# Second layer of a two-layer sequence model: one PSUM bank for the sums, step sizes ahead of the gates, small GpSimd operations on ScalarE, another order on the way to the experts

## The reference, cut to what matters

```python
# selective scan (d_model 256, d_inner 512, 16 states), per sequence
x_ssm, res = split(x @ W_in.T)                      # 512 + 512
x_ssm = silu(conv4(x_ssm) + b_conv)
B_C   = (x_ssm @ W_x.T)[..., 512:]                  # 16 values a token
dt    = softplus(x_ssm @ W_dt.T + b_dt)             # step size
h     = exp(dt * A) * h + dt * B * x_ssm            # scan over tokens, 512 x 16 states
y     = h.sum(-1) + D * x_ssm
out   = (y * silu(res)) @ W_out.T
# sorted experts: two groups of 32 experts, top 2 of each group
xs = x2[tokens sorted by expert]
ys = (silu(xs @ wg[e]) * (xs @ wu[e])) @ wd[e]      # 256 -> 128 -> 256
out = zeros.at[tok].add(ys * weight)                # both groups, averaged
```

## Time and profile before

| | us |
|---|---|
| median of 3 runs | 4872.82 (4868.73 to 4875.76) |
| the profiled execution | 4861.3 |
| its span in the trace | 4859.5 |
| TensorE matmul busy | 4278.9 (88%) |
| VectorE busy | 3722.3 (77%) |
| GpSimd busy | 3037.6 (63%) |
| ScalarE busy | 2516.5 (52%) |

### The profile page before, as it was taken

How to read it: one execution, slowest core, us unless ns; L and a number is a source line. 1 busy time by engine, 2 the same in 40 slices (tenths; PEclk the granted TensorE clock), 3 DMA queues, 4 the chain that set the end, 5 groups by cost and what they waited for, 6 DMA issues and landing times. The chain is left out here.

```text
span 4859.5 us, 59293 instructions
## 1 busy us (share of the span) xinstructions
PE 4278.9 (88%) x19350; PEld 2834.2 (58%) x19350; DVE 3722.3 (77%) x5916; ACT 2516.5 (52%) x4871; POOL 3037.6 (63%) x1970
## 2 busy tenths in 40 slices
PE   5689999999999999998988889888988888499993
PEld 1355555555556655565655566555655665388883
DVE  6887777778788878775149988888988898555676
ACT  1344334334333434433468777777777777155552
POOL 3455555555555545554158889888888888555552
PEclk7899999999999999999999999999999999699997
DMA  4233332333332333333112221111222111496787
GB/s 146 80 107 104 109 100 92 110 98 111 109 104 90 105 105 104 105 109 100 39 67 75 80 73 70 70 69 69 86 87 75 69 67 68 162 248 209 260 282 278
DMA packets 304193, 545.54 MB, mean 112 GB/s; under 512 B 31504, under 2 KB 148496, under 8 KB 294928
## 3 DMA queue, kind: packets, MB, share of 16 engines
q1 hardware_dynamic: 276240, 466.09, 29.5%
q0 software_dynamic: 27648, 75.67, 4.3%
HBM read 422.72 MB, written 118.92 MB: 111 GB/s over the span
## 5 line engine op out<-in xcount | busy, mean ns | idle before, releaser
L1456 POOL TENSOR_TENSOR c_dbx<-c_dtx,c_Brep 128x1024 f32<-128x1024 f32 x512 | 1200.5, 2362 | 167.8 <-DVE c_hs L1474 57.5
L876 POOL TENSOR_TENSOR a_kv<-a_rk,a_kv 128x512 f32<-128x512 f32 x512 | 807.7, 1589 | 402.9 <-DMA a_kv<-v_rows 402.6
L1474 DVE TENSOR_TENSOR_SCAN c_hs<-psum,c_carry,c_dbx 128x512 f32<-128x512 f32 x768 | 937.4, 1266 | 120.6 <-ACT psum L1463 68.0
L885 DVE TENSOR_TENSOR_SCAN a_S<-a_decay,a_carry,a_kv 128x513 f32<-128x513 f32 x512 | 795.1, 1553 | 185.4 <-POOL a_kv L876 94.4
L1463 ACT ACTIVATE psum<-c_dt,c_cols 128x512 f32<-128x512 f32 x1024 | 698.9, 689 | 402.6 <-DVE c_hs L1474 398.0
L802 POOL TENSOR_TENSOR a_hid_e<-a_hid_e,a_g_rep 128x512 f32<-128x512 f32 x256 | 386.7, 1513 | 773.3 <-ACT a_hid_e L791 596.9
L1490 PEld LDWEIGHTS psum<-ident,c_hs 128*128 128x128 f32 x4096 | 488.2, 144 | 394.5 <-DVE c_hs L1474 217.5
L1490 PE MATMUL psum<-ident,c_hs 128*128 128x128 f32 x4096 | 612.0, 282 | 114.1 <-DVE c_hs L1474 109.9
L891 DVE TENSOR_TENSOR a_prod<-a_rk,a_S 128x512 f32<-128x512 f32 x512 | 547.3, 1069 | 68.4 <-PE psum L907 68.4
L783 PE MATMUL psum<-a_W_down,a_hid_e 128*128 128x256 f32 x2304 | 552.0, 385 | 52.7 <-POOL a_hid_e L802 28.5
L207 PE MATMUL psum<-a_xT,a_W_up 128*128 128x512 f32 x1152 | 559.2, 615 | 15.1 <-ACT a_hid_e L791 15.0
(11 more groups left out here) (271 smaller groups left out, 6777.5 us busy)
## 6 DMA issues: line engine op xcount, KB each, us to landing
a_kv<-v_rows SPq DMA_DIRECT2D x512, 256.0 KB
a_g_rep<-g_rows SPq DMA_DIRECT2D x256, 256.0 KB, 3.9
c_Brep<-b_rows SPq DMA_DIRECT2D x64, 1024.0 KB, 4.7
d_xs<-sorted_rows SPq DMA_DIRECT2D x320, 128.5 KB
d_w<-results SPq DMA_DIRECT2D x64, 512.0 KB, 11.4
d_w<-in_d_experts SPq DMA_DIRECT2D x32, 768.0 KB, 8.8
sorted_rows<-d_zeros SPq DMA_DIRECT2D x66, 128.5 KB, 6.2
a_xa<-in_L_attn_x SPq DMA_DIRECT2D x16, 512.0 KB, 4.7
```

Of the source, the lines that this page charges most:

```text
L876: m_kv[g] = pool.mark(nc.gpsimd.tensor_tensor(kv[:, g % NV, 1:C + 1], rk[slot][:, 1, hb, :], kv[:, g % NV, 1:C + 1], ALU.mult))
L885: m_scan[q] = dve.mark(nc.vector.tensor_tensor_scan(S[:, q % NS, :], decay[cq % 2][:, hb, :], kv[:, q % NV, :], carry[:, sq_:sq_ + 1], ALU ...
L1456: m_dbx[g] = m_dbx[g + 1] = pool.mark(nc.gpsimd.tensor_tensor(dbx[:, r:r + 2, :], dtx[slot][:, e, :].unsqueeze(1).broadcast_to([P, 2, C]), ...
L1474: m_scan[q] = dve.mark(nc.vector.tensor_tensor_scan(hs[:, q % NR, :], psum[:, DA + q % ND, :], dbx[:, q % NX, :], first, ALU.mult, ALU.add))
```

## The change

The shared banks of layer1_phase become four (0 to 3), the three for exp(dt*A) move to 4 to 6, and bank 7 alone holds the sums; the gating product is issued two scans behind the last one of a block, and TensorE waits for it ahead of the next block's sum. The root of the norm is exp(-0.5 * ln(v)) on ScalarE. The row numbers are changed by ScalarE. xs is declared done ahead of the gates, so that sizes can begin; the step sizes e=1 to 3 wait for the B rows to be issued. For the last chunk, the first three blocks are transposed and multiplied with W_out while the scans still run (turned_early), and the last block behind them (last_product); its rows for the second choice go out of a copy (again, in the place of dbx) with their own row numbers, so that its 16 scatters are issued one behind the other, group by group, each group with its own semaphore. All 16 pairs of the first group's weights and the plan are fetched when the scans have ended; SyncE waits for the last chunk's scatters of one group at a time; the second block of pads goes over ScalarE's queue, the third behind the first six tiles.

```diff
@@ layer1_phase: tensors, banks
-        pre, tmp = soon("pre", [P, EB, C + KC - 1]), soon("tmp", [P, 2, C])
+        tmp = soon("tmp", [P, 2, C])
...
+        pre = soon("pre", [P, EB, C + KC - 1])
...
-        NR, NX, DA, ND = 8, 6, 3, 3
+        s_last = [sem(f"last_of_group{g}") for g in range(GR)]
+        NR, NX, DA, ND = 8, 6, 4, 3
...
-        G, YB = Banks(psum, 0, 3), 6
-        G.freed = [*bank_marks, "held"]
+        G, YB = Banks(psum, 0, 4), 7
+        G.freed = [*bank_marks, "held", "held"]
@@ normalise
             act.after(m)
-            act.mark(nc.scalar.activation(rstd[:, :], mv[:, :, 1], ACT.Identity, bias=eps[:, 0:1]))
-            m = buf["read"] = act.mark(nc.scalar.activation(shift[:, :], mv[:, :, 0], ACT.Identity, scale=-1.0))
+            m = act.mark(nc.scalar.activation(rstd[:, :], mv[:, :, 1], ACT.Ln, bias=eps[:, 0:1]))
+            m_mean = buf["read"] = act.mark(nc.scalar.activation(shift[:, :], mv[:, :, 0], ACT.Identity, scale=-1.0))
+            act.after(m)
+            m = act.mark(nc.scalar.activation(rstd[:, :], rstd[:, :], ACT.Exp, scale=-0.5))
             yield from pause(POOL_LAG - 1)
-            pool.after(m)
-            m = pool.mark(nc.gpsimd.tensor_tensor(rstd[:, :], rstd[:, :], neghalf[:, 0:TL], ALU.pow))
-            pool.after(m)
+            pool.after(m, m_mean)
             m = pool.mark(nc.gpsimd.tensor_tensor(shift[:, :], shift[:, :], rstd[:, :], ALU.mult))
@@ main
                 yield
+            m_done["xs", c] = list(m_xs.values())
             while c >= 2 and not is_done(("y", c - 2)):
                 yield
...
             m_done["stored", c] = True
             yield from gates(2)
             m_done["gate", c] = m_gate[TL - 1]
-            m_done["xs", c] = list(m_xs.values())
@@ sizes
 
             def step_size(e):
+                while e >= 1 and not is_done(("stored", c)):
+                    yield
                 i, bank = yield from G.claim(pe)
@@ after_scan
             products = []
-            for half in range(2):
-                i, bank = yield from G.claim(pe)
-                pe.after(*marks)
...
+            else:
+                products = yield from last_product(c)
...
-            marks = yield from transposed(xn_, yT, KB, m_xn, [])
+            if c >= 2:
+                m_done["row", c] = act.mark(nc.scalar.activation(xn_[:, :, D], xn_[:, :, D], ACT.Identity, bias=two_chunks[:, 0:1]))
+            yield
+            marks = yield from transposed(xn_, yT, KB, m_xn, [m_done.get(("yT free", c - 1))])
             m_done["xn free", c] = marks[-1]
+            if c == NCH - 1:
+                act.after(m_done["scanned", c][0], m_done["scanned", c][1])
+                dve.after(m_done["scanned", c][0])
+                m_done["copied", c] = [act.mark(nc.scalar.copy(again[:, t, 0:D], xn_[:, t, 0:D])) for t in range(TL)]
+                m_done["copied", c].append(dve.mark(nc.vector.tensor_scalar(again[:, :, D], token_row[:, :], float(c * C * TOP + 1), None, ALU.add)))
...
@@ new, beside sort_rows
+        def turned_early(c):
+
+            marks = m_done["turned", c] = []
+            for e in range(EB - 1):
+                while not is_done(("gated", c, e)):
+                    yield
+                i, bank = yield from G.claim(pe)
+                pe.after(m_done["gated", c, e])
+                for t in range(TL):
+                    m = nc.tensor.transpose(bank[:, t * P:(t + 1) * P], gate[c % 2][:, t, e * P:(e + 1) * P], ident[:, :])
+                m = pe.mark(m)
+                yield from pause(LAG)
+                act.after(m, m_done["conv", c])
+                marks.append(act.mark(nc.scalar.copy(pre[:, e, 0:C], bank)))
+                G.freed[i] = marks[-1]
+                yield
+            while not is_done(("placed", c - 1)):
+                yield
+            banks = m_done["products", c] = []
+            for half in range(2):
+                i, bank = yield from G.claim(pe)
+                banks.append((i, bank))
+                pe.after(*marks)
+                for t in range(2):
+                    at = (2 * half + t) * P
+                    for e in range(EB - 1):
+                        nc.tensor.matmul(bank[:, t * D:(t + 1) * D], pre[:, e, at:at + P], W_out[:, e, :], start=(t == 0 and e == 0), stop=False, skip_group_check=True)
+                    yield
+            m_done["begun", c] = True
+
+        def last_product(c):
+
+            e = EB - 1
+            while not is_done(("begun", c)):
+                yield
+            i, bank = yield from G.claim(pe)
+            pe.after(m_done["gated", c, e])
+            for t in range(TL):
+                m = nc.tensor.transpose(bank[:, t * P:(t + 1) * P], gate[c % 2][:, t, e * P:(e + 1) * P], ident[:, :])
+            act.after(pe.mark(m))
+            m_y = G.freed[i] = act.mark(nc.scalar.copy(pre[:, e, 0:C], bank))
+            pe.after(m_y)
+            products = []
+            for half, (i, bank) in enumerate(m_done["products", c]):
+                for t in range(2):
+                    at = (2 * half + t) * P
+                    m = nc.tensor.matmul(bank[:, t * D:(t + 1) * D], pre[:, e, at:at + P], W_out[:, e, :], start=False, stop=(t == 1), skip_group_check=True)
+                products.append((i, bank, pe.mark(m)))
+            return products
@@ sort_rows
                 yield
             yield from pause(POOL_LAG)
-            m_row = None
-            if c >= 2:
-
-                pool.engine.wait_ge(s_sorted[c % 2], c // 2 * per_chunk)
-                m_row = pool.mark(nc.gpsimd.tensor_tensor(route.xn[c % 2][:, :, D], route.xn[c % 2][:, :, D], two_chunks[:, :], ALU.add))
+            m_row = m_done["row", c]
+            if c == NCH - 1:
+                pool.after_alone(*m_done["placed", c], *m_done["copied", c], m_row)
+                for g in range(GR):
+                    for k in range(TOP):
+                        for t in range(TL):
...
+                m_done["sorted", c] = True
+                return
             pool.after_alone(*m_done["placed", c], m_row)
             for k in range(TOP):
                 if k:
 
-                    yield from pause(POOL_LAG)
-                    pool.engine.wait_ge(s_sorted[c % 2], c // 2 * per_chunk + per_chunk // TOP)
-                    pool.after_alone(pool.mark(nc.gpsimd.tensor_tensor(route.xn[c % 2][:, :, D], route.xn[c % 2][:, :, D], ones[:, 0:TL], ALU.add)))
+                    yield from pause(POOL_LAG - 2)
+                    act.engine.wait_ge(s_sorted[c % 2], c // 2 * per_chunk + per_chunk // TOP)
+                    m_row = act.mark(nc.scalar.activation(route.xn[c % 2][:, :, D], route.xn[c % 2][:, :, D], ACT.Identity, bias=ones[:, 0:1]))
+                    yield
+                    pool.after_alone(m_row)
@@ scans
                         sort.append(sort_rows(c - 1))
-                    if c + 1 < NCH:
-                        ahead.append(main(c + 1))
+                    ahead.append(main(c + 1) if c + 1 < NCH else turned_early(c))
...
+                q = g - AHEAD - 2
+                if 0 <= q < total and q % N == N - 1:
+                    cq, sq = divmod(q, steps)
+                    e = sq // N
+                    background.drain(until=lambda: is_done(("gate", cq)))
+                    dve.after(m_sum[q], m_done["gate", cq])
+                    m_done["gated", cq, e] = m_done["y free"] = dve.mark(nc.vector.tensor_tensor(
+                        gate[cq % 2][:, :, e * P:(e + 1) * P], psum[:, YB, :].rearrange("p (t d) -> p t d", t=TL),
+                        gate[cq % 2][:, :, e * P:(e + 1) * P], ALU.mult))
...
                     if n == 0:
-                        pe.after(m_done.get(("y free", e % 2)))
+                        pe.after(m_done.get("y free"))
                         for t in range(TL):
-                            nc.tensor.matmul(psum[:, YB + e % 2, t * P:(t + 1) * P], xs[cq % 2][:, e, t * P:(t + 1) * P], skip_diag[:, e, :],
+                            nc.tensor.matmul(psum[:, YB, t * P:(t + 1) * P], xs[cq % 2][:, e, t * P:(t + 1) * P], skip_diag[:, e, :],
...
-                q = g - AHEAD - 6
-                if 0 <= q < total and q % N == N - 1:
...
@@ end of layer1_phase
+        G.freed[3] = None
...
+        again = dbx[:, 0:3, :].rearrange("p a c -> p (a c)")[:, 0:TL * Z.width].rearrange("p (t w) -> p t w", t=TL)
...
-        route.sorted = s_sorted, NCH // 2 * per_chunk
+        route.sorted = [(s_sorted[(NCH - 2) % 2], NCH // 2 * per_chunk), (s_sorted[(NCH - 1) % 2], (NCH // 2 - 1) * per_chunk)]
+        route.sorted_last = [(s_last[g], per_chunk // GR) for g in range(GR)]
@@ sorted_experts_phase
-        LATE = 8
+        LATE, EARLY = 8, 16
...
         sp.after(*route.scanned)
-        EARLY = 6
+        nc.sync.dma_start(plan, I["d_plan"]).then_inc(s_plan, 16)
         for n in range(EARLY):
             fetch_weights(0, n)
 
-        s_stored, s_sorted = route.ended, route.sorted
```

(25 more changed lines are left out.)

49 lines of the change are left out of this document (26 added, 23 removed).

## The result

The changed kernel takes 4822.65 us (median of 6, 4817.24 to 4833.76) where the kernel before took 4873.56 beside it (median of 6): ratio 0.989 (95% interval 0.988 to 0.990), 51 us or 1.1% faster. The forecast was 4800. It fell short by 23 us. The profiled execution took 4822.83 us, its span 4821.0.

What follows compares the result with a forecast made beforehand. No engine was full in the scans; VectorE's gaps mostly ended with GpSimd's products. Loop 45 plus way 28 made 73 us off the profiled 4861.3; with the median 11.5 higher, the forecast was 4800 us, range 4770 to 4835.

Steps and rivals of the forecast that it cites:

- The loop: Second-layer scans: 3 us a chunk less, taken over 15 chunks, 45 us.
- GpSimd's share: Scan loop: without powers and row-number updates GpSimd has 3.7 us a chunk less, shrinking VectorE's gaps behind it.
- Step sizes and banks: Scan loop: gains of 2.5 and 1.5 us a chunk in two scatter stretches, minus 1.5 for the single sum bank.
- The single sum bank: Block ends in the scans: VectorE waits at the gate for TensorE's sum, 1.5 us a chunk.
- rival C: Block ends: VectorE and TensorE wait for each other at every gate, from 6.5 us a chunk no gain; slower, chance 0.08.
- A: Scan loop stays as it was, only the way to the experts pays: 4845 us, chance 0.26.
- B: Scan loop: all GpSimd gaps close and gates are free, 99.6 us a chunk, 4729 us, chance 0.10.
- D: Root on ScalarE costs two table loads per normalisation: 4862 us, no measurable change, chance 0.06.
- The way: From last scan to first expert matmul: 28 us less, at most 34, 18 if ScalarE's wait is long.
- The last quarter of products: Way to the experts: a quarter of transposes and products plus copy and addition remain after the scans, 7.5 us less.
- Root and small gaps: Way to the experts: root on ScalarE saves the power and some place behind scatters, about 2 us.
- ScalarE's wait: Way to the experts: ScalarE waits for chunk 14's first half of scatters to land, 0 to 7 us, taken as 3.5.

Runs made afterwards that it cites:

- experiment 1: Kernel before with the banks alone: four shared PSUM banks, one for sums, gating two scans behind; 4893.71 us, ratio 1.0042.
- experiment 2: Kernel before with only the step sizes moved ahead of the gates; 4898.16 us, ratio 1.0048.
- experiment 3: Kernel before with only roots and row numbers moved from GpSimd to ScalarE; 4869.30 us, ratio 0.9987.
- experiment 5: Changed kernel without the step sizes ahead of the gates; 4870.23 us, ratio 0.9980.
- experiment 7: Changed kernel with VectorE's addition of the output products five turns of the background stream later; 4886.85 us, ratio 1.0013.
- experiment 8: Changed kernel with the addition three turns later, router and ranks kept in place, chunk 14's second row-number update on GpSimd; 4834.75 us, ratio 0.9905.
- experiment 9: Changed kernel without the four D-term matmuls at each gate, so TensorE has less work; 4819.74 us, ratio 0.9863.
- experiment 11: Changed kernel with chunk 14's second row-number update back on GpSimd; 4826.07 us, ratio 0.9885.
- experiment 12: Changed kernel with eight early weight pairs, pads ahead of fetches, last mean product on VectorE, chunk 14's second row-number update on GpSimd; 4835.79 us, ratio 0.9907.
- experiment 10: Changed kernel with two sum banks and four shared, two exponential banks, scans one step behind exponentials, gating six scans behind; 4944.47 us, ratio 1.0118.
- experiment 4: Changed kernel with banks and step-size order as before, keeping roots and row numbers on ScalarE and the new way; 4838.37 us, ratio 0.9926.
- experiment 6: Changed kernel with the banks as before (three shared, two for sums); 4867.58 us, ratio 0.9972.

## Why the prediction was right, and where it was not

**The sum.** Faster by 51 us, inside the forecast's own range of 4770 to 4835. The 23 us that lack are 16 of the loop and 7 of the way; the tail, taken at nothing, stayed within 2 us of its length in experiments 1 to 3.

**The loop: 29 instead of 45.** The middle thirteen chunks went from 106.5 to 103.9 us, 2.6 of the 3 foreseen (I had said 104). The first chunk grew from 100.5 to 106.2 and the last from 94.7 to 96.2: over fifteen chunks, counted from the last gate of one to that of the next (the first is from chunk 0's to chunk 1's), 2.6 x 13 - 5.7 - 1.5 = 26.6. The step that failed is the factor of 15, more than the 3: I measured one chunk in the middle and took the first and the last to be the same. In the runs the longer first chunk goes with the four banks: 104.7 to 107.8 us in experiments 1, 5, 7, 8, 9, 11, 12 and the changed kernel (111.3 in 10), 101.5 to 102.0 in 2, 3, 4 and 6. Why wasn't looked for.

**GpSimd's share** was right as a mechanism. Powers and updates gone brought 16 us of scans by themselves (experiment 3), with GpSimd's wait for the first step size still there (50.6 us in experiment 4, whose scans are those of 3); that wait went with the other two parts, as foreseen. But experiments 1 and 2 took it down to 7.5 and 9.9 us and got slower, so that the gain I drew from GpSimd's earlier start has no run to stand on.

**Step sizes and banks** were priced as separate terms, 2.5 + 1.5 and -1.5 a chunk. The runs don't bear separate prices. Alone each makes the kernel 20 to 24 us slower, on top of the other parts 26 and 23 us of scans, and together they gain 13. My sum held 2.5 a chunk for them, of which 1.1 was the powers' and updates' part, so 1.4 or 21 us. Roots and row numbers gave 16 us where the sum held 1.1 + 0.5 a chunk, 24. Both terms came out too high, by 8 each. That the term for banks and step sizes was no further off is luck: it added a gain and a price that no run shows alone.

**The single sum bank, rival C.** The danger was real and put in the wrong place. In the changed kernel the gate waits 0 and the addition 5 us a chunk; in experiment 1 gate, addition and ranks (13.8 us) wait 6.6 a chunk together, which is C's limit of 6.5, and that kernel is 0.4% slower; in experiment 5 they are 7.5. Experiments 7 and 8 show the wait wandering between addition, gate and ranks with the order of the background. I should have asked at every meeting of VectorE with TensorE, and not only at the one that the diff moves.

**Rivals A, B, D.** A said that the loop stays; the scans got 29 us shorter, and experiment 4 has 16 of them. B wanted all gaps closed, 99.6 us a chunk: it was 103.9. D wanted table loads at the root, and ScalarE's timeline of the last chunk has none: the three activations (L1043, L1044, L1046) start at 4153.69, 4153.90 and 4154.02, and over the 13 chunks loads stand at the same four places of main as before.

**The way: 21 instead of 28.** Four terms make the difference of 7.1. The last quarter of products brought 5.7, not 7.5: from the end of the gate (4145.28) to the last addition's end (4151.64) are 6.4 us, against my 4.5. I had taken a quarter of the old time, but TensorE's clock was another. Granted clock (third column from the right) over the products, before and after:

```profile
4178.00:4185.70 7.70, 6.98 (x32) 5.80 (x31) 1.37 (x2) 0.00 (x0) 4.32 (x6) 1.00 0.22 75
```

```profile
4147.00:4151.00 4.00, 3.78 (x8) 2.52 (x8) 0.74 (x2) 0.07 (x1) 0.00 (x0) 0.50 0.00 0
```

Before, 32 products took 7.15 us at the 2.4 GHz level, behind 16 transposes. Now TensorE is idle in part for the last scans (1.50 of 4 us busy from 4140 to 4144), and the 8 products that are left run at 1.2 GHz in 3.78 us: a quarter of the work in half of the time. Root and small gaps did 0.9 better (2.9 us, of which 0.4 is an earlier gate). ScalarE's wait cost 5.6, not 3.5, for I saw GpSimd's scatters ahead of the mean product and not those behind it. And from the first group's last scatter to the fetch it took 4205.03 - 4196.75 = 8.3 us, 7.3 until SyncE's wait was over (4204.04) and 1.0 for the register load, where I had put 2.5 to 5.3 from stretches with less traffic: the fetch came 19.3 us after placing, not 15.2. In sum 1.8 - 0.9 + 2.1 + 4.1 = 7.1. A sentence of the prediction is wrong besides: that no weight load stands in front of the pads. All sixteen stood in front of them on SyncE's queue. Here it cost little, since the pads landed at 4203.6 and the scatters at 4203.2; in experiment 11 it cost 7.3 us. The DMA engines of the changed kernel in that stretch:

```profile
4160.00:4190.00 30.00, 11.63 (x49) 9.10 (x48) 12.83 (x61) 1.83 (x6) 12.48 (x13) 0.50 1.03 404
4195.00:4200.00 5.00, 0.00 (x0) 0.00 (x0) 3.20 (x13) 0.00 (x0) 3.78 (x5) 0.50 1.14 185
```

Weights end at about 4192; from then to 4200 scatters and pads alone keep the engines full, at half the rate. How long the first group's landing takes wasn't separated from what moves beside it: from the last of the eight scatters' end to the last landing event it is 3.5 us in experiment 4, 3.7 in 12, 4.6 in 11 and 6.5 in the changed kernel. By the Trainium skill, DMA: Bandwidth & Descriptors, section Queues, rings and completion order, the rows of several queues are served in turn, so weights should not hold back scatters by more than their share. The trace agrees that they were not held for all of the load: chunk 14's first half landed 5.6 us after its last issue ended (4162.48 to 4168.11), while the engines moved 404 GB/s, most of it weights. But I had drawn from it that landings under load are short, and 6.5 us with pads beside them doesn't bear that out.

**The tiles** lost little but not nothing:

```profile
4211.52 4.38 SPq L1916 DMA_DIRECT2D sorted_rows<-d_zeros  x8
4216.09 2.56 SPq L1929 DMA_DIRECT2D d_xs<-sorted_rows  x4
...
4221.05 0.44 PE L2010 MATMUL psum<-ident,d_xs 128*128 128x128 f32 x2 [3.25 <-DMA d_xs<-sorted_rows]
```

Eight pads stand in SyncE's queue ahead of the seventh tile's rows, and TensorE waits 3.25 us. In experiment 4 the same place costs 4.76. The eight kernels with the new way that keep sixteen early pairs and three exponential banks have a tail of 615.4 to 627.4 us, 623 in the mean; the kernel before has 604.7 and the three experiments with the old way 613.9 to 617.9. So an earlier start gives back 7 us behind it in the mean, each profile being one execution; how many of the 7 are the pads' wasn't tried alone.

What stays open: why both parts together end at 1641 and not lower, that is, which order of the background would put TensorE's results in front of every meeting. Experiment 9 says it isn't mainly the amount of work, 8 says that one stage moved alone only moves the wait, and what part the granted clock has in experiments 2, 6 and 7 is open too.

## What to carry to other kernels

Where several engines are 75 to 90% busy and a hand-written order feeds them all, two parts of a change can each lose alone and win together, so price and test them as a pair, and for each engine list every place at which it waits for another, not the one that the diff touches. A chunk measured in the middle is no measure of the first and the last. A wait for a landing belongs on an engine whose queue has nothing urgent behind it, and a small store that a fetch waits for belongs on a DMA queue with nothing large ahead of it. Where a fetch waits for several landings, and for its own engine's issues, look at each before one is named.

## What the runs showed of the hardware

Rows of about 1 KB, scattered or stored, kept the sixteen DMA engines busy at 185 GB/s (share 1.14, 4195 to 4200 in the changed kernel) and 212 (share 0.85, 4186 to 4201 in experiment 12); the stretch of the weights moved 404 (share 1.03). Stores issued behind the weights on SyncE's queue landed at 4210.8 in experiment 11, stores issued at the same time on ScalarE's queue at 4204.1. Within the expert tiles TensorE shows gaps of 1.9 to 2.7 us, one in before's profile and three in most others (at 4416.76, 4499.55 and 4599.08 in the changed kernel, 2.51, 2.30 and 2.36 us), at nearly the same distance from the first tile and with a different engine named each time; their cause wasn't looked for. Two of them, some 4.7 us, are part of what before's profile lacks behind the first expert matmul. The two functions of the root ran without a table load, 0.28, 0.19 and 0.21 us for the three small activations, against 1.04 us for the power on GpSimd.
